# Attention and an int8 feed-forward layer on eight cores: three x buffers and later projection batches

## The reference

```python
def _layernorm(x, axis=-1, eps=1e-5):
    m = jnp.mean(x, axis=axis, keepdims=True)
    v = jnp.var(x, axis=axis, keepdims=True)
    return (x - m) / jnp.sqrt(v + eps)

# attention: x [8, 2048, 1024], Wk, Wq, Wv [1024, 1024]
K = x @ Wk
Q = x @ Wq
V = x @ Wv
scores = einsum('bnd,bmd->bnm', Q, K) / sqrt(1024)
scores = where(causal, scores, -inf)
attn = softmax(scores) @ V

# feed-forward: weight_q int8 [1024, 1024], EPS = 1e-6
amax = max(abs(x2d), axis=-1, keepdims=True)
x_scale = maximum(amax, EPS) / 127.0
x_q = clip(round(x2d / x_scale), -128, 127)
acc = x_q @ weight_q.T
out = acc * x_scale * weight_scale[None, :] + bias

# the whole
x = x + attention(_layernorm(x))
x = x + feed_forward(_layernorm(x))
```

## Time and profile before

| | us |
|---|---|
| runs (three) | 588.0, 588.6, 590.61; median 588.6 |
| profiled execution, its own time | 587.79 |
| its span, slowest core (core 7) | 586.0 |
| spans of the other cores | 579.8 to 582.7 |
| PE busy | 406.5 (69%) |
| DVE busy | 250.1 (43%) |
| ACT busy | 172.3 (29%) |
| POOL busy | 81.2 (14%) |

### The profile page before, as it was taken

How to read it: one execution, slowest core, us unless ns; L and a number is a source line. 1 busy time by engine, 2 the same in 40 slices (tenths; PEclk the granted TensorE clock), 3 DMA queues, 4 the chain that set the end, 5 groups by cost and what they waited for, 6 DMA issues and landing times.

```text
span 586.0 us, 5963 instructions; the slowest of 8 cores (579.8 to 586.0 us)
## 1 busy us (share of the span) xinstructions
PE 406.5 (69%) x2008; PEld 189.6 (32%) x2008; DVE 250.1 (43%) x425; ACT 172.3 (29%) x304; POOL 81.2 (14%) x44
## 2 busy tenths in 40 slices
PE   0000899379937996997465666887789877988654
PEld 0000344234423443443222233333444433434211
DVE  2112434444344344343634455544655545435320
ACT  3222400241024102000433444344553446244220
POOL 3000000000000000000222233322313313111311
PEclk9999999779977997999577799888999999989866
DMA  8999200220022000002202222220122120220000
GB/s 147 184 198 265 73 1 0 72 68 7 0 71 73 1 1 2 0 1 95 84 2 71 73 72 72 74 70 21 54 73 72 73 73 0 73 72 1 36 36 36
DMA packets 11453, 35.07 MB, mean 60 GB/s; under 512 B 896, under 2 KB 896, under 8 KB 11424
## 3 DMA queue, kind: packets, MB, share of 16 engines
q1 hardware_dynamic: 6912, 25.17, 12.7%
q0 software_dynamic: 4512, 9.54, 8.9%
HBM read 31.56 MB, written 8.39 MB: 68 GB/s over the span
## 4 chain that ended last, share of the span: by engine, by line
PE 56%; DVE 15%; ACT 10%; DMA 9%; issue 8%; DVEq 1%; POOLq 0%; ACTq 0%; SPq 0%
PE psF L191 30%; PE psF L468 10%; DMA xbuf<-x 9%; PE psF L571 9%; PE psF L360 7%; DVE st L510 2%; DVE x L580 2%; ACT xnbuf L227 2%; DVE st L371 2%; DVE st L399 2%; DVE st L379 2%; ACT xqf L555 1%; ACT xqT L440 1%; ACT AT_sb L544 1%; DVE st L403 1%
## 5 line engine op out<-in xcount | busy, mean ns | idle before, releaser
L468 PE MATMUL psF<-wqt_sb,xqT 128*128 128x512 bf16 x256 | 76.8, 467 | 46.1 <-ACT xqT L440 34.0
L571 PE MATMUL psF<-Vt,AT_sb 128*128 128x512 bf16 x272 | 67.4, 406 | 22.9 <-ACT AT_sb L544 9.2
L191 PE MATMUL psF<-xnT,wq_sb 128*128 128x512 bf16 x256 | 62.7, 411 | 22.2 <-DVE xnT L275 22.2
L360 PE MATMUL psF<-KT,QT 128*128 128x512 bf16 (+3 forms) x320 | 63.6, 356 | 0.9 <-DVE Vt L206 0.9
L496 POOL TENSOR_TENSOR outf<-t,x1b 128x1024 f32<-128x1024 f32 x16 | 37.6, 2349 | 153.3 <-DVE t L492 153.3
L235 PE MATMUL psBF<-ident_sb,xnbuf 128*128 128x128 bf16 x128 | 12.1, 257 | 66.4 <-ACT xnbuf L227 66.4
L468 PEld LDWEIGHTS psF<-wqt_sb,xqT 128*128 128x128 bf16 x256 | 28.4, 115 | 89.5 <-issue 74.1
L191 PE MATMUL psF<-xnT,wk_sb 128*128 128x512 bf16 x256 | 55.9, 379 | 0.0
L191 PE MATMUL psF<-wv_sb,xnT 128*128 128x512 bf16 x256 | 55.9, 379 | 0.0
L251 DVE TENSOR_REDUCE st<-xbuf 128x1 f32<-128x1024 f32 x16 | 19.5, 1218 | 70.0 <-DMA xbuf<-x 70.0
L587 POOL TENSOR_TENSOR x1b<-x,bb_sb 128x1024 f32<-128x1024 f32 x16 | 37.6, 2349 | 79.4 <-DVE x L580 73.4
(11 more groups left out here) (57 smaller groups left out, 378.5 us busy)
## 6 DMA issues: line engine op xcount, KB each, us to landing
xbuf<-x SPq DMA_DIRECT2D x16, 512.0 KB, 3.8
xr<-x SPq DMA_DIRECT2D x16, 512.0 KB, 4.0
y<-outf SPq DMA_DIRECT2D x16, 512.0 KB, 2.9
wq_sb<-wq POOLq DMA_DIRECT2D x1, 2048.0 KB, 21.4
wk_sb<-wk POOLq DMA_DIRECT2D x1, 2048.0 KB, 35.0
wv_sb<-wv POOLq DMA_DIRECT2D x1, 2048.0 KB, 48.3
wqt_sb<-wqt POOLq DMA_DIRECT2D x1, 2048.0 KB, 54.5
wsb_sb<-wsb POOLq DMA_DIRECT2D x1, 512.0 KB, 5.4
```

The lines of the kernel that those rows point to most:

```text
L191: (lambda t: t.matmul(psQ(b), lhsT, rhs, start=st, stop=sp)))()
L360: (lambda te: te.matmul(score_ap(b, n), lhsT, rhs, start=st, stop=sp)))()
L468: (lambda te: te.matmul(psMM[:, sl * 512:(sl + 1) * 512], xqT[jpar][:, kc * 128:(kc + 1) * 128], wqt[:, kc * D + sl * 512: kc * D + (sl + ...
L571: fn = (lambda jj=jj, sl=sl, st=st, sp=sp: (lambda te: te.matmul(psMM[:, sl * 512:(sl + 1) * 512], AT_sb[:, jj * 128:(jj + 1) * 128], Vt[: ...
```

## The change

- `xbuf` gets a third buffer, with a semaphore of its own (`dx2`); tile t goes to buffer t % 3 and is loaded after the normalisation and the sum of tile t - 3. The small statistics tile `st1` gets four buffers in place of two.
- A setting of the program builder, `dynamic_dma_scratch_size`, is put to 8192 bytes; `xqf` gets one buffer in place of two, and its writer waits for the reader of the tile before.
- The projections of the first four tiles are put on TensorE after the copy of tile 7 in place of tile 3, those of the next four after tile 11 in place of 7, and the third and fourth batch one behind the other after tile 15. `flush_evacs` stands at h = 8 and 12 and after the loop.
- The loads of wqt and of the mask stand after the loop in the program text.
- attn x V waits for the first half of `AT_sb` and for L492 at its first matmul, and for the second half at the first matmul that reads it.

```diff
+    nc = bass.Bass("TRN2", target_bir_lowering=False,
+                   dynamic_dma_scratch_size=8192)
...
-    st1 = [at(f"st1_{i}", [128, 16], F32) for i in range(2)]
+    st1 = [at(f"st1_{i}", [128, 16], F32) for i in range(4)]
...
-    xbuf = [at(f"xbuf{i}", [128, D], F32) for i in range(2)]
+    xbuf = [at(f"xbuf{i}", [128, D], F32) for i in range(3)]
...
-    xqf = [at(f"xqf{i}", [128, D], F32) for i in range(2)]
+    xqf = at("xqf", [128, D], F32)
...
-        m_wqt = sch.op("gpsimd", dma(
-            wqt[:].rearrange("p (c d) -> p c d", d=D),
-            wqt_h.rearrange("(c p) d -> p c d", p=128)), inc="dwt", inc_by=16)
-        m_mask = sch.op("gpsimd", dma(mask[:], mask_h), inc="dwm", inc_by=16)
...
-                if t >= 2:
-                    w = [("ss", m_xn[t - 2]), ("vs", m_red[t - 2])]
+                if t >= 3:
+                    w = [("ss", m_xn[t - 3]), ("vs", m_red[t - 3])]
                 m_dx[t] = sch.op("sync",
-                                 dma(xbuf[par][:], x_h[t * 128:(t + 1) * 128, :]),
-                                 inc=f"dx{par}", inc_by=16, waits=w)
+                                 dma(xbuf[xpar][:], x_h[t * 128:(t + 1) * 128, :]),
+                                 inc=f"dx{xpar}", inc_by=16, waits=w)
...
-            if 0 <= h < NT and h % 4 == 0 and h >= 4:
+            if h in (8, 12):
                 flush_evacs(10 ** 9)
...
-                if h % 4 == 3:
-                    s4 = h // 4
+                batches = {7: [0], 11: [1], 15: [2, 3]}.get(h, [])
+                for s4 in batches:
                     for c in range(KC):
-                        emit_qkv_group("q", c, s4, m_evT[h])
+                        emit_qkv_group("q", c, s4, m_evT[s4 * 4 + 3])
                     for c in range(KC):
-                        emit_qkv_group("k", c, s4, m_evT[h])
+                        emit_qkv_group("k", c, s4, m_evT[s4 * 4 + 3])
...
         flush_evacs(10 ** 9)
         assert g_ctr[0] == n_groups_total
+        m_wqt = sch.op("gpsimd", dma(
+            wqt[:].rearrange("p (c d) -> p c d", d=D),
+            wqt_h.rearrange("(c p) d -> p c d", p=128)), inc="dwt", inc_by=16)
+        m_mask = sch.op("gpsimd", dma(mask[:], mask_h), inc="dwm", inc_by=16)
...
-                    inc="ss", waits=[("vs", m_inv[h]), ("vs", m_rnd.get(h - 2, 0))])
+                    inc="ss", waits=[("vs", m_inv[h]), ("vs", m_rnd.get(h - 1, 0))])
...
-                w = [("ss", m_evATb[i]), ("ss", m_evATa[i]),
-                     ("vs", m_stt2.get(i - 2, 0))]
-                first = True
+                ha_av = (nch + 1) // 2
                 for jj in range(nch):
+                    if jj == 0:
+                        w = [("ss", m_evATa[i]), ("vs", m_stt2.get(i - 2, 0))]
+                    elif jj == ha_av:
+                        w = [("ss", m_evATb[i])]
+                    else:
+                        w = ()
...
-                                         waits=(w if first else ()))
-                        first = False
+                                         waits=(w if sl == 0 else ()))
```

More of the change, by code:

```diff
@@ L23 @@
 ENGINES = ("sync", "gpsimd", "tensor", "vector", "scalar")
-SEMS = ("dx0", "dx1", "dr0", "dr1", "do0", "do1",
+SEMS = ("dx0", "dx1", "dx2", "dr0", "dr1", "do0", "do1",
         "dwi", "dwq", "dwk", "dwv", "dwt", "dwm", "dws", "dwb",
@@ L53, in build_nc @@
 def build_nc():
-    nc = bass.Bass("TRN2", target_bir_lowering=False)
+    nc = bass.Bass("TRN2", target_bir_lowering=False,
+                   dynamic_dma_scratch_size=8192)
     x_h = nc.dram_tensor("x", [S, D], F32, kind="ExternalInput").ap()
@@ L213, in build_nc @@
                 par = h % 2
-                stt = st1[par]
+                stt = st1[h % 4]
                 sch.op("scalar", (lambda stt=stt: (lambda s: s.activation(
@@ L226, in build_nc @@
                 m_b2 = sch.cnt["ss"]
-                m_xn[h] = sch.op("scalar", (lambda par=par, stt=stt: (lambda s: s.activation(
-                    xnbuf[par][:], xbuf[par][:], AF.Identity,
+                m_xn[h] = sch.op("scalar", (lambda par=par, hx=h % 3, stt=stt: (lambda s: s.activation(
+                    xnbuf[par][:], xbuf[hx][:], AF.Identity,
                     scale=stt[:, 5:6], bias=stt[:, 6:7])))(),
@@ L242, in build_nc @@
                 par = t % 2
-                stt = st1[par]
+                xpar = t % 3
+                stt = st1[t % 4]
                 w = []
-                if t >= 2:
-                    w = [("ss", m_xn[t - 2]), ("vs", m_red[t - 2])]
+                if t >= 3:
+                    w = [("ss", m_xn[t - 3]), ("vs", m_red[t - 3])]
                 m_dx[t] = sch.op("sync",
-                                 dma(xbuf[par][:], x_h[t * 128:(t + 1) * 128, :]),
-                                 inc=f"dx{par}", inc_by=16, waits=w)
+                                 dma(xbuf[xpar][:], x_h[t * 128:(t + 1) * 128, :]),
+                                 inc=f"dx{xpar}", inc_by=16, waits=w)
                 m_red[t] = sch.op(
-                    "vector", (lambda par=par, stt=stt: (lambda v: v.reduce_sum(
-                        stt[:, 0:1], xbuf[par][:], axis=AX.X)))(),
-                    inc="vs", waits=[(f"dx{par}", m_dx[t])])
+                    "vector", (lambda xpar=xpar, stt=stt: (lambda v: v.reduce_sum(
+                        stt[:, 0:1], xbuf[xpar][:], axis=AX.X)))(),
+                    inc="vs", waits=[(f"dx{xpar}", m_dx[t])])
                 sch.op("vector", (lambda stt=stt: (lambda v: v.tensor_scalar(
@@ L261, in build_nc @@
                 m_mm = sch.cnt["vs"]
-                m_sq = sch.op("scalar", (lambda par=par, stt=stt: (lambda s: s.activation(
-                    junk[:], xbuf[par][:], AF.Square,
+                m_sq = sch.op("scalar", (lambda xpar=xpar, stt=stt: (lambda s: s.activation(
+                    junk[:], xbuf[xpar][:], AF.Square,
                     accum_out=stt[:, 2:3])))(),
-                    inc="ss", waits=[(f"dx{par}", m_dx[t]), ("ss", m_junkw[0])])
+                    inc="ss", waits=[(f"dx{xpar}", m_dx[t]), ("ss", m_junkw[0])])
                 m_junkw[0] = m_sq
@@ L554, in build_nc @@
             if 0 <= h < NT:
-                m_xqf[h] = sch.op("scalar", (lambda hpar=hpar, hst=hst: (lambda s: s.activation(
-                    xqf[hpar][:], xn1[:], AF.Identity, scale=hst[:, 14:15])))(),
-                    inc="ss", waits=[("vs", m_inv[h]), ("vs", m_rnd.get(h - 2, 0))])
+                m_xqf[h] = sch.op("scalar", (lambda hst=hst: (lambda s: s.activation(
+                    xqf[:], xn1[:], AF.Identity, scale=hst[:, 14:15])))(),
+                    inc="ss", waits=[("vs", m_inv[h]), ("vs", m_rnd.get(h - 1, 0))])
                 m_rnd[h] = sch.op("vector", (lambda hpar=hpar: (lambda v: v.tensor_scalar(
-                    xq[hpar][:], xqf[hpar][:], C_RND, C_RND,
+                    xq[hpar][:], xqf[:], C_RND, C_RND,
                     ALU.add, ALU.subtract)))(),
```

## The result

The changed kernel takes 545.8 us in the median, against 588.6 for the kernel before beside it: a ratio of 0.9267 [0.9249, 0.9284] (in brackets the 95% interval). Predicted were 549 and a range of 538 to 565. The profiled execution took 545.02 us with a span of 543.2 on its slowest core, 3; the slowest of before was core 7 with 586.0.

The account below looks back on a forecast made before the run. The prediction took the chain as 56% TensorE and 9% x loads. Gains of 7.0 + 6.9 + 8.1 + 9.35 + 4.3 + 3.7 = 39.4 us off 587.79 gave 548.4, median 549, range 538 to 565.

Parts of the forecast that it names:

- hole one: Gap on TensorE between the first and second projection batches: 16.4 us falls to 9.5, 6.9 gained.
- the attention: Attention rounds: split copy wait gains 4.3 us in rounds 11 to 15, a kept clock 3.7 in rounds 13 to 15.
- the start: Stretch before the first projection batch: two x loads in flight move its start from 60.77 to 53.8, 7.0 us gained.
- Rival (a): Before the first batch: two loads in flight take turns, 8.6 us per tile; total 562; chance 12%.
- The V weights: Weight load beside the first x loads: lands by 53, wanted at 84, so nothing counted.
- Hole two: Gap on TensorE between the second and third projection batches: 15.3 us falls to 7.2, 8.1 gained.
- Hole three: Gap on TensorE between the third and fourth projection batches: disappears, 8.25 us gained.
- the slow start: Beginning of the fourth projection batch: its loss against matmuls at full clock disappears, 1.1 us gained.
- First two batches: Projection matmuls of tiles 0 to 7: same matmuls as before, so no gain or loss counted.
- The evacuations: VectorE reaches them some 9 us into a batch; TensorE's six banks leave a us or three of cover.
- rival (b): Attention rounds: that part gives nothing, by another engine ending the round or the clock falling; total 557; chance 12%.
- Rival (c): Long stretch of the last two batches: the clock doesn't hold, up to 633 if all 384 matmuls slow; chance 3%.

Follow-up runs that it names:

- e2: Kernel before with the third x buffer and what belongs to it, but old batch places and old attn x V wait: 552.9 us, ratio 0.9376.
- e3: Kernel before with the shifted projection batches alone, two x buffers and the old attn x V wait: 587.05 us, ratio 0.9960.
- e1: Kernel before with only the split wait of attn x V on the two halves of AT_sb: 580.7 us, ratio 0.9839.
- e5: Changed kernel with the projection batches put back to tiles 3, 7, 11 and 15: 544.25 us, ratio 0.9221.
- e7: Changed kernel without the batch shift, wk and the loads behind it held until tile 5 of x has landed: 542.7 us, ratio 0.9196.
- e6: Changed kernel with wk and the loads behind it on POOL held until tile 8 of x has landed: 541.3 us, ratio 0.9158.
- e8: Changed kernel with batches behind tiles 5, 9, 13 and 15, and wk held until tile 6 has landed: 536.2 us, ratio 0.9091.
- e9: Changed kernel with batches behind tiles 5, 9, 13 and 15, and wk released when tile 4 has landed: 536.7 us, ratio 0.9093.
- e4: Kernel before with only the smaller descriptor memory, one xqf and the wqt and mask loads moved later: 589.7 us, ratio 1.000.
- e10: Changed kernel with its first batch held until the mask, the last load on POOL, has landed: 558.5 us in a single execution.

## Why the prediction was right, step by step

The sum was right to 3 us, and each of its terms to some 5. All gains are core 7 before against core 3 after, unless a mean is named. That the sum is closer than its terms is luck in part: hole one and the attention gave more than was said, the start and the batches less. By the mean over the eight cores the start gives 6.8 (7.0 said), the holes 25.9 (23.3), the matmuls of the batches 0.2 (1.1) and the attention 7.8 (8.0).

- **The start**: 53.8 predicted, 55.36 measured in the chain (the eight cores 52.9 to 55.6 in the timeline), a gain of 5.4 for 7.0. The mechanism is the one given: two loads in flight, each as long as before or a little longer (8.1 to 10.8). Rival (a), loads in turn, wanted 67 (69 by its own 8.6 a tile, counted from tile 3's 20.9) and falls. The V weights, counted to land by 53, took 58.2 from their issue; they are wanted 30 us into the batch, so that cost nothing.
- **Hole one** was mis-read. The prediction let its batch wait for tile 11's copy and came to 9.5. The batch that stands there is that of tiles 4 to 7, and it asks only for the copy of tile 7; the copy of tile 11 ends 2.4 after the batch begins. Measured 7.2, a gain of 9.2 for 6.9. The 9.5 is what the hole measures where the batch does need its own last tile, in e2.
- **Hole two**: 7.2 predicted and measured. **Hole three**: gone; with the 1.1 of the slow start 9.35 was claimed, and 94.1 for the last two batches and the hole, less 85.35, is 8.75.
- **First two batches** were said to stay as they are. They are 0.9 and 0.6 longer (the first 45.13 against the 44.22 of the earlier trace rows). For the first it is the grant of 0.81: the four cores that have it take 45.3 to 46.3 for the batch in the timeline, the four others 42.4 to 44.0. What is known of its cause is in the last section. The second starts at a grant of 0.52 for 4.5 us, where before it was 0.70 for 4.75. The evacuations gave no wait here; they did in e3.
- The terms up to the attention give 29.95 (from 274.40 to 244.45) for 31.35.
- **The attention**: 311.6 - 298.75 = 12.85 for 8.0. The idle ahead of attn x V falls by 3.7 in rounds 11 to 15, for which 4.3 was predicted, and by 0.8 in rounds 8 to 10, where nothing was. The clock held in three of three rounds: 7.87, 8.32 and 8.77 became 6.20, 6.63 and 7.08, which is 5.05 for the 3.7 of two rounds. That is core 7, one of three cores that lost the clock in all three rounds before; the other five lost it in one. In the changed kernel and in e1 no core loses it in any. Nearly all of the remaining 3.3 lies in rounds 0 to 7, where nothing was claimed, and is a matter of which core is compared: this part took 129.0 to 132.2 on the cores of before, 132.2 on core 7, the most, and 129.1 on core 3 after. By the mean over the cores the whole stage goes from 307.3 to 299.5, 7.8. Alone (e1) the split wait gives 8.55 by the medians, 1.6% [1.2, 2.1]; rival (b) falls.
- **Rival (c)**, the clock in the long batch, falls: 85.35 for 384 where the full clock has 84. The prediction named a grant under 1.00 in this stretch as a sign of being wrong, and it is 0.97; but the loss stands in the first 4.8 us, at 0.50, and after them 373 matmuls run at 1.00, so the length takes nothing. The Trainium skill's rule that dense matmuls on three or more cores of a die are held to 13/16 (TensorE: Matmul & The Clock Gate, Seeing it yourself) is not seen in this stretch; 0.81 is 13/16, and it does appear on whole dies, for some 14 us of the first batch.

What the prediction left out is that its parts don't add. Alone, by the medians, they give 36.4 (third buffer), 8.55 (wait) and 2.2 (shift), 47.1 together; the three at once give 42.8. The first two do add up: 6.2% and 1.6% alone, 7.8% together (e5). It is the shift that doesn't. Beside the third buffer it pays for three more tiles at the start and gets it back later: from e2 to the changed kernel, by the mean over the cores in the timeline, the start comes 17.9 later (36.1 to 54.0), the holes give back 13.4 and the matmuls 2.6, so that attention begins 1.9 later. Each step of the sum was set against the kernel before; the third buffer without the shift, which is as fast or faster, wasn't priced.

## What to carry to other kernels

Where a batch is moved behind later tiles, read from the wait lists which tile each batch still asks for; the hole is set by that tile and not by the last one before it. A prefetch and a reordering that hide the same wait should be priced together and one by one, because the second may only hand back what the first saved. And a load that nobody wants yet costs what flies beside it: holding it moved the start by 5 us (e7) and 11 us (e6) here, and its own lateness then took back all of that (e7) or nearly half (e6).

## What the runs showed of the hardware

An x load of 512 KB takes 8 to 11 us while the weight loads are queued and 3.3 to 4.4 when they are held back (e6, e7, e8); much of the difference stands in the earlier trace rows: the first 4 us move no x at all. A weight load of 2 MB with no other ahead of it takes 21 to 26 us from its issue: wq 21.4 before and 25.5 in the changed kernel, the held wk 23.0 to 26.1 in e6 to e9. Queued one behind the other, in the changed kernel's DMA issues, the next lands 16 us after the last:

```profile
wq_sb<-wq POOLq DMA_DIRECT2D x1, 2048.0 KB, 25.5
wk_sb<-wk POOLq DMA_DIRECT2D x1, 2048.0 KB, 41.6
wv_sb<-wv POOLq DMA_DIRECT2D x1, 2048.0 KB, 58.2
```

A granted clock of 0.81 shows in every kernel whose first batch lies beside the weight loads (the changed one, e2, e5 to e9), some 11 to 16 us after the start of the batch: on one die for up to 15 us, in most of them on the other too for 3 to 5, and in e6, where TensorE soon waits for K, on two cores for 3 to 4. It shows in none where the batch comes after them (before, e1, e3, e4, e10). e2 for example, core 3, beside 258 GB/s:

```profile
50.00:62.00 12.00, 12.00 (x48) 4.95 (x46) 3.77 (x6) 0.00 (x0) 0.00 (x0) 0.81 1.14 258
```

In the changed kernel it comes 11 us into the batch, when most of the loads are over: the row of core 3 has 76 GB/s, the ten us before it 326 at a grant of 1.00. From 70 to 80 us no load moves anything on core 3, and the grant stays:

```profile
70.00:80.00 10.00, 10.00 (x39) 4.13 (x38) 3.23 (x5) 0.94 (x5) 0.00 (x0) 0.81 0.00 0
```

That it is gone where the batch comes after the loads, e10 shows in one execution, and the traces of before, e1, e3 and e4 agree. By what the loads bring it about, why it outlasts them, and why one die has it for longer than the other, or alone, stays open.
